# Row scatter and row gathers issued column by column behind block pairs, and second-half routing begun ahead of the first pair

## The chip, the cores and the metric

The kernel runs on one core of a Trainium2 chip. Its engines work side by side and wait for each other on semaphores: TensorE (PE, matrix multiplies), VectorE (DVE) and ScalarE (ACT, elementwise work), GpSimd (POOL), and SyncE (SP), which here only issues DMAs. GpSimd issues DMAs too, the indirect ones, whose row addresses come out of a table in on-chip memory. The metric is device time in microseconds of one execution; it is given as the median of three timed runs.

## The reference, cut to what matters

Two mixture-of-experts (MoE) feed-forwards stand before and behind a two-layer retention block. In all three the input is normalised first.

```python
def moe(hidden):                          # 4096 tokens of 256
    flat = hidden.reshape(4096, 256)
    probs = softmax(flat @ router_w + router_bias)     # 16 experts
    top_w, top_i = top_k(probs, 2)
    norm_w = top_w / (sum(top_w) + 1e-6)
    combine = sum(one_hot(top_i, 16) * norm_w[..., None], axis=1)
    routed = combine[:, 15:16] * flat                  # expert 15 is the identity
    for e in range(15):
        y = silu(flat @ gate_w[e]) * (flat @ up_w[e]) @ down_w[e]
        routed = routed + combine[:, e:e + 1] * y
    gate = causal_conv(hidden, conv_w)                 # 3 taps
    shared = silu(gate) * (hidden @ shared_up_w) @ shared_down_w
    return shared + routed

x = x + 0.5 * moe(layernorm(x))
x = x + retention_block(layernorm(x))     # 2 layers: projections, retention, feed-forward
x = x + 0.5 * moe(layernorm(x))
```

## The kernel before, in words

One program does both MoE layers and the retention block between them. Tiles of the first MoE have names that begin with `a_`, those of the second with `b_`, those of the retention block with `l_`; the code of the two MoE layers is the same. `x_sb` holds the activations on the chip.

An MoE layer works on its 4096 tokens in two halves of 16 columns; a column is 128 tokens, one to a partition. **Routing** of a half takes softmax and top-2 on DVE, then counts on PE (`count`, 17 small matmuls in one accumulation behind a clearing one) how many tokens each expert has, and DVE works out of the counts at which row of a DRAM buffer (`rows`) each token is to stand, so that the tokens of one expert lie side by side in blocks of 128 rows. The result is the index table `pos_i`, and the semaphore `placed` says that it is there. For the second half this runs as a generator `later` of seven pieces (plan, plan, place, place, weigh, block table, block table), of which DVE takes one behind the work of each block pair.

**Scatter.** GpSimd writes each column of normalised tokens twice (top-2) into `rows`, one indirect DMA for each: 32 for a half, L804. That of the second half waits only for `placed` and for the buffer's clearing.

**Block pairs.** The experts' work is a loop of 46 pairs of blocks; pairs 0 to 22 are of the first half, 23 to 45 of the second. For pair n: SP loads it (`load_block`, L470, four pairs ahead), PE transposes it (`turn_x`, L1284, two pairs ahead), ACT and DVE split it into a high and a low part (L650, L1009), PE multiplies it by the gate and up weights in three passes (`gateup`, L83 to L85, into `gu_ps`), ACT applies the gate (L658), DVE forms the product (`product`, L1017, whose semaphore is `h_done`), PE transposes the product (L1305), ACT and DVE split it (L664, L1023), PE does the down projection of it one pair later, ACT copies the result out of PSUM (`take_y`, L670), and SP stores it into `rows` (`store_y`, L476). ACT's `take_y` of a pair waits until the store of the pair two before it has left the buffer.

SP is one queue in order. In iteration q it issues the load of pair q+4 and then the store of pair q-3. The load of pair 23, the first of the second half, waits for all the second half's scatters; behind it on SP stand the load's own iteration's store, that of pair 16, and all that follows. In the first MoE, SP's queue also holds stores of weights (`low_dram`) in iterations 28 to 42 and three stores of `x`.

**Gathers ("picks").** When all stores of the first half have landed, GpSimd gathers the results of column c, two indirect DMAs each (L813), into a ring of 8 columns (6 in the second MoE), and DVE adds them into `x_sb` (`combine`, L1029), one column behind the product of each pair from n = 28 (`COMBINE_FROM`) on. From the ring's length on, a pick waits until `combine` has freed its slot.

So each engine's order is written out by hand, and what the change touches is: GpSimd's second scatter and its picks of the first half, DVE's order around `low_x(0)` and `low_x(1)` (which lead to the first product), and PE's order around `turn_x(0)`.

## Time and profile before

| what | value |
|---|---|
| median of 3 timed runs | 1405.84 us (1404.09 to 1406.28) |
| the profiled execution: its span | 1579.5 us |
| busy in the profiled span: PE | 1351.4 us (86%) |
| DVE | 1011.0 us (64%) |
| ACT | 614.6 us (39%) |
| POOL | 571.9 us (36%) |
| HBM traffic over the span | 95 GB/s |

The table puts two different things side by side. The time by which the kernel is judged is the first line. All durations and starts of single instructions come from one execution under the profiler, and that one took 173.7 us longer than the median. "Released by" in the profile is the instruction or DMA on whose semaphore an engine waited last. The end of a matmul is modelled; that of the other engines' instructions is recorded. PE is busy for most of the span; what follows is read in stretches, for the two MoE parts and the part between have different limits.

### The profile page before, as it was taken

The page shows a single profiled execution, that of the slowest core. Times are in us where ns is not written, and L with a number is a line of the kernel's source. Part 1 is how long each engine was busy: PE and PEld are TensorE (multiplying, and loading weights), DVE is VectorE, ACT ScalarE, POOL GpSimd, SP SyncE. Part 2 cuts the span into 40 slices and gives each one's busy share as a digit, 9 for nine tenths or more (in the row PEclk, how much of TensorE's full clock was granted, in tenths as well). Part 3 has the DMA queues.
Part 4 walks back from the last instruction along what each step waited for, and adds up shares of the span by engine and source line. Part 5 has one row for each costly group of instructions (what it writes and reads, how often), then busy time and mean ns, then how long its engine had stood idle before and what let it go on. Part 6 is the DMA issues. An engine that isn't in the chain of part 4 may idle for free.

```text
span 1579.5 us, 30698 instructions
## 1 busy us (share of the span) xinstructions
PE 1351.4 (86%) x11824; PEld 1104.9 (70%) x11824; DVE 1011.0 (64%) x2391; ACT 614.6 (39%) x1034; POOL 571.9 (36%) x460
## 2 busy tenths in 40 slices
PE   6871968876999999999998999999999676496885
PEld 3461968644788888888886888888887446496753
DVE  5661536658977877777768778797787453253623
ACT  5630635422333433343344334424455262263410
POOL 0726033352342323224424443364343704304252
PEclk9975979989999999999999999999999788698998
DMA  9963559650000000000010000000002463355542
GB/s 326 372 213 122 174 175 321 206 190 23 28 2 2 1 2 1 1 2 32 8 58 1 1 15 2 15 15 14 2 28 89 167 229 131 124 181 171 156 150 90
DMA packets 113867, 151.63 MB, mean 96 GB/s; under 512 B 12224, under 2 KB 96192, under 8 KB 113728
## 3 DMA queue, kind: packets, MB, share of 16 engines
q1 hardware_dynamic: 99328, 114.02, 21.8%
q0 software_dynamic: 12288, 33.57, 6.6%
q8 instruction: 99, 1.62, 0.4%
q10 hardware_dynamic: 2112, 2.10, 0.4%
q14 instruction: 40, 0.33, 0.1%
HBM read 78.21 MB, written 71.43 MB: 95 GB/s over the span
## 4 chain that ended last, share of the span: by engine, by line
PE 53%; DVE 16%; another core or an unknown queue 8%; issue 2%; ACT 2%; POOL 0%; DVEq 0%; ACTq 0%
PE l_w_ps L83 8%; PE l_w_ps L85 7%; PE l_w_ps L84 7%; DVE l_probs L2221 4%; PE l_banks L2505 3%; PE l_rm_ps L2537 2%; PE l_banks L83 2%; PE l_banks L84 2%; PE l_banks L85 2%; DVE l_f_lo L2252 2%; PE l_rm_ps L2530 2%; DVE l_full L2174 1%; PE b_gu_ps L83 1%; PE b_t_ps L1284 1%
## 5 line engine op out<-in xcount | busy, mean ns | idle before, releaser
L2221 DVE TENSOR_TENSOR l_probs<-l_banks,l_past 128x512 f32<-128x512 f32 x256 | 160.1, 684 | 29.8 <-PE l_banks L2505 29.7
L1964 ACT ACTIVATE l_act_f<-l_w_ps,l_ffn_b 128x512 f32<-128x512 f32 x120 | 82.7, 690 | 169.0 <-PE l_w_ps L85 163.9
L83 PE MATMUL l_w_ps<-l_w_hi,l_f_hi 128*128 128x256 f32 x496 | 143.6, 290 | 2.6 <-DVE l_f_lo L2252 2.4
L84 PE MATMUL l_w_ps<-l_w_lo,l_f_hi 128*128 128x256 f32 x496 | 139.6, 281 | 0.0
L85 PE MATMUL l_w_ps<-l_w_hi,l_f_lo 128*128 128x256 f32 x496 | 139.5, 281 | 0.0
L2059 POOL TENSOR_TENSOR l_g_lo<-l_q,l_g_hi 128x1024 fp32r<-128x1024 f32 x16 | 39.1, 2447 | 266.9 <-ACT l_g_hi L1955 266.9
L813 POOL DMA_INDIRECT b_picked<-rows,b_pos_i x64 | 61.1, 955 | 137.4 <-DMA rows<-b_yb 88.5
L83 PE MATMUL l_w_ps<-l_b_hi,l_w_hi 128*128 128x512 f32 x240 | 102.2, 426 | 0.3 <-ACT l_f_hi L1965 0.3
L83 PEld LDWEIGHTS l_w_ps<-l_w_hi,l_f_hi 128*128 128x128 f32 x496 | 93.3, 188 | 8.8 <-issue 8.7
L2252 DVE TENSOR_TENSOR l_f_lo<-l_act_f,l_f_hi 128x512 fp32r<-128x512 f32 x128 | 85.9, 703 | 18.5 <-ACT l_f_hi L1965 18.4
L2046 POOL TENSOR_TENSOR l_q_wide<-l_q,l_pair_mask 128x1024 f32<-128x1024 f32 x32 | 60.1, 1899 | 103.7 <-DVE l_q L2189 100.0
L804 POOL DMA_INDIRECT rows<-a_xn,a_pos_i x64 | 66.3, 1036 | 83.9 <-DVE a_pos_i L969 64.9
L85 PE MATMUL l_w_ps<-l_b_hi,l_w_lo 128*128 128x512 f32 x240 | 94.7, 394 | 0.0
L84 PE MATMUL l_w_ps<-l_b_lo,l_w_hi 128*128 128x512 f32 x240 | 94.5, 394 | 0.0
L84 PEld LDWEIGHTS l_w_ps<-l_w_lo,l_f_hi 128*128 128x128 f32 x496 | 93.5, 188 | 0.0
L85 PEld LDWEIGHTS l_w_ps<-l_w_hi,l_f_lo 128*128 128x128 f32 x496 | 93.4, 188 | 0.0
L1965 ACT ACTIVATE l_f_hi<-l_w_ps,l_ffn_b 128x512 fp32r<-128x512 f32 x120 | 81.8, 681 | 0.0
L1943 ACT ACTIVATE l_std<-l_mv,eps 128x4 f32<-128x4 f32 x47 | 13.6, 298 | 174.4 <-DVE l_mv L2144 170.7
L2537 PE MATMUL l_rm_ps<-l_probs,l_v_wide 128*32 128x128 f32 x2048 | 78.9, 275 | 2.8 <-DVE l_v_wide L2210 2.8
L2067 POOL TENSOR_TENSOR x_sb<-x_sb,l_bias 128x1024 f32<-128x1024 f32 x32 | 77.2, 2414 | 0.0
L2505 PE MATMUL l_banks<-l_q_wide,l_kT 32*128 32x256 f32 x1024 | 74.2, 401 | 1.0 <-POOL l_q_wide L2046 1.0
L2154 DVE TENSOR_SCALAR l_xn<-x_sb,l_mv,l_rstd 128x256 f32<-128x256 f32 x128 | 69.8, 606 | 1.2
(432 smaller groups left out, 4053.0 us busy)
## 6 DMA issues: line engine op xcount, KB each, us to landing
rows<-a_zeros SPq DMA_DIRECT2D x14, 1024.0 KB, 10.7
a_xb<-rows SPq DMA_DIRECT2D x46, 256.0 KB
rows<-a_yb SPq DMA_DIRECT2D x46, 256.0 KB
b_xb<-rows SPq DMA_DIRECT2D x46, 256.0 KB
rows<-b_yb SPq DMA_DIRECT2D x46, 256.0 KB
a_w_in<-in_moe_w SPq DMA_DIRECT2D x15, 384.0 KB, 10.2
low_dram<-a_w_lo SPq DMA_DIRECT2D x15, 384.0 KB
b_w_lo<-low_dram SPq DMA_DIRECT2D x15, 384.0 KB
```

What stands on the lines that cost most here:

```text
L83: tensor.matmul(out, w_hi, x_hi, start=start, stop=False)
L84: tensor.matmul(out, w_hi, x_lo, start=False, stop=False)
L85: return tensor.matmul(out, w_lo, x_hi, start=False, stop=stop)
L804: pool.indirect_dma_start(own_rows[b], bass.IndirectOffsetOnAxis(ap=pos_i[:, b, k, c:c + 1], axis=0), normal(START[b] + c), None).then_inc ...
L1964: nc.scalar.activation(act_f[:, f, :], hidden_ps(b, f), ACT.Gelu, bias=ffn1_b[:, b.layer, f:f + 1]).then_inc(act_done, 1)
L1965: nc.scalar.activation(f_hi[:, f, :], hidden_ps(b, f), ACT.Gelu, bias=ffn1_b[:, b.layer, f:f + 1]).then_inc(f_hi_done, 1)
L2067: pool.tensor_tensor(tile, tile, bias[:, row:row + 1, :].broadcast_to([P, SUB, D]), ALU.add).then_inc(done, 1)
L2154: last = dve.tensor_scalar(dst(s), tile_of(t, s), mv[:, s, 0:1], rstd[:, s:s + 1], ALU.subtract, ALU.mult)
L2221: dve.tensor_tensor(probs[c % 2][:, r * w:(r + 1) * w].rearrange("p (h n) -> p h n", n=P), banks[:, r, :].rearrange("p (h n) -> p h n", n= ...
L2252: dve.tensor_tensor(f_lo[:, f, :], act_f[:, f, :], f_hi[:, f, :].bitcast(F32), ALU.subtract).then_inc(f_lo_done, 1)
L2505: last = pe.matmul(banks[:, r, g * PH * P:(g + 1) * PH * P], kT[rows, g, t], q_wide[rows, g, :, t], start=True, stop=True)
L2537: last = pe.matmul(ret_ps[r * QUAD:(r + 1) * QUAD, g * P:(g + 1) * P], v_wide[:, c, g * NQ + r, i:i + PH, :].rearrange("p i x -> p (i x)") ...
```

## The change

Three edits, the same in both MoE layers.

1. GpSimd's scatter of column c of the second half waits for `h_done` of 2 + 19c//16. The semaphore counts finished products, so the 16 columns stand behind products 1, 2, 3, 4, 5, 6, 8, 9, 10, 11, 12, 14, 15, 16, 17 and 18.
2. GpSimd's pick of column c of the first half waits for `h_done` of 27 + 18c//16: behind products 26, 27, 28, 29, 30, 31, 32, 33, 35, 36, 37, 38, 39, 40, 41 and 42. The order of DVE's `combine` is as it was: column c behind product 28+c.
3. The count of the second half on PE moves from behind `turn_x(2)` of pair 0 to ahead of `turn_x(0)`. DVE takes the two plan pieces ahead of `low_x(0)` and `low_x(1)`, then two pieces of `later` for each of the first two pairs and one after that, so that `placed` of the second half comes behind product 0 and not behind product 3.

```diff
+            def paced_scatter(c):
+                pool.wait_ge(h_done, 2 + (PAIR0[1] - 4) * c // PARTS[1])
+
+            def paced_pick(c):
+                pool.wait_ge(h_done, COMBINE_FROM - 1 + (NPAIRS - COMBINE_FROM) * c // PARTS[0])
+
             def scatter(b):
                 pool.wait_ge(placed, b + 1)
...
                 for c in range(PARTS[b]):
+                    if b == 1:
+                        paced_scatter(c)
                     for k in range(2):
...
                 own = c - START[b]
+                if b == 0:
+                    paced_pick(c)
                 for k in range(2):
...
                 later = rest()
+            next(later)
             low_x(0)
+            next(later)
             low_x(1)
...
                 low_h(n)
-                next(later, None)
+                for _ in range(2 if n < 2 else 1):
+                    next(later, None)
...
                 shared_in(2)
+            count(1)
             if begins:
                 pe.wait_ge(dve_lo_done, PIECES)
             turn_x(0)
...
                 if n + 2 < NPAIRS:
                     turn_x(n + 2)
-                if n == 0:
-                    count(1)
```

What stands in a row on GpSimd, in the first MoE, from the first half's scatter on. Before (32 scatters of the first half, 32 of the second, then the picks; the waits are the semaphores' names):

```order
L804 DMA rows<-a_xn,a_pos_i 7936x256 [waits a_cleared0,a_placed]
L804 DMA rows<-a_xn,a_pos_i 7936x256 x31
L804 DMA rows<-a_xn,a_pos_i 7936x256 [waits a_cleared1,a_placed]
L804 DMA rows<-a_xn,a_pos_i 7936x256 x31
L813 DMA a_picked<-rows,a_pos_i 128x256 [waits a_scattered11,y_kept0,a_scattered10,y_kept1,a_scattered01,a_scattered00]
L813 DMA a_picked<-rows,a_pos_i 128x256 x15
L813 DMA a_picked<-rows,a_pos_i 128x256 [waits a_x_done]
L813 DMA a_picked<-rows,a_pos_i 128x256
```

Now (the lines L804 and L813 are L812 and L823), the same stretch up to the second half's third column:

```order
L812 DMA rows<-a_xn,a_pos_i 7936x256 [waits a_cleared0,a_placed]
L812 DMA rows<-a_xn,a_pos_i 7936x256 x31
L812 DMA rows<-a_xn,a_pos_i 7936x256 [waits a_h_done,a_cleared1,a_placed]
L812 DMA rows<-a_xn,a_pos_i 7936x256
L812 DMA rows<-a_xn,a_pos_i 7936x256 [waits a_h_done]
L812 DMA rows<-a_xn,a_pos_i 7936x256
L812 DMA rows<-a_xn,a_pos_i 7936x256 [waits a_h_done]
L812 DMA rows<-a_xn,a_pos_i 7936x256
```

Each column is now two DMAs behind a wait of its own, and the picks read likewise: two DMAs behind `a_h_done`, from the ninth column on behind `a_h_done,a_x_done`.

PE at the start of the second MoE's pairs, before: `shared_in(2)` (L415, L420), then the transposes of pairs 0 and 1 (L1284), then the shared expert's down projection (L427). (In the second MoE the waits carry semaphore names of the first, which are used again; `a_cleared0` here is the one that says that DVE has finished `b_both`, the routing's picks.)

```order
L1230 MATMUL b_low_ps<-ident,b_lgT_last 128x128 x3
L415 MATMUL b_gu_ps<-b_xT_first,b_w_sh 128x512 [waits a_low_kept,a_weight_in9,a_weight_in10]
L415 MATMUL b_gu_ps<-b_xT_first,b_w_sh 128x512 x5
L420 MATMUL b_gu_ps<-b_xT_first,b_w_sh 128x512 x2
L1284 MATMUL b_t_ps<-ident,b_xb 128x128 [waits a_weight_in10,a_halo_done]
L1284 MATMUL b_t_ps<-ident,b_xb 128x128 x3
L1284 MATMUL b_t_ps<-ident,b_xb 128x128 [waits a_weight_in10,a_xT_done]
L1284 MATMUL b_t_ps<-ident,b_xb 128x128 x3
L427 MATMUL b_acc_ps<-b_w_sh,b_sh 128x256 [waits a_zeroed,a_low_kept]
```

Now (L1240 is L1253, L1284 is L1297):

```order
L415 MATMUL b_gu_ps<-b_xT_first,b_w_sh 128x512 x5
L420 MATMUL b_gu_ps<-b_xT_first,b_w_sh 128x512 x2
L1253 MATMUL b_low_ps<-b_blank,b_ones 128x255 [waits a_cleared0]
L1254 MATMUL b_low_ps<-b_both,b_tri 128x240
L1256 MATMUL b_low_ps<-b_both,b_ones 128x240
...
L1256 MATMUL b_low_ps<-b_both,b_ones 128x15
L1297 MATMUL b_t_ps<-ident,b_xb 128x128 [waits a_weight_in10,a_halo_done]
L1297 MATMUL b_t_ps<-ident,b_xb 128x128 x3
L1297 MATMUL b_t_ps<-ident,b_xb 128x128 [waits a_weight_in10,a_xT_done]
```

The count, with its wait for `b_both`, now stands ahead of the first pair's transposes.

DVE at the same place of the first MoE, before (L1009 is `low_x`, L1017 the product, L1023 `low_h`, L947 to L949 the first plan piece):

```order
L1003 SCALAR_TENSOR_TENSOR x_sb<-a_acc_ps,x_sb 128x1024 [waits a_s_acc_done]
L1009 TENSOR_TENSOR a_bx_lo<-a_t_ps,a_bx_hi 128x512 [waits a_x_hi_done] x2
L1017 TENSOR_TENSOR a_bh<-a_bg,a_gu_ps 128x256 [waits a_gate_done]
L1009 TENSOR_TENSOR a_bx_lo<-a_t_ps,a_bx_hi 128x512 [waits a_gu_done,a_x_hi_done]
L1023 TENSOR_TENSOR a_bh_lo<-a_low_ps,a_bh_hi 128x256 [waits a_h_hi_done]
L947 TENSOR_SCALAR a_nb_i<-a_low_ps 128x15 [waits a_pre_done]
```

Now (each line ten higher):

```order
L1013 SCALAR_TENSOR_TENSOR x_sb<-a_acc_ps,x_sb 128x1024 [waits a_s_acc_done]
L957 TENSOR_SCALAR a_nb_i<-a_low_ps 128x15 [waits a_pre_done]
L958 TENSOR_SCALAR a_nb_i<-a_nb_i 128x15 [waits a_route_step]
L959 CAST a_nb<-a_nb_i 128x15 [waits a_route_step]
L1019 TENSOR_TENSOR a_bx_lo<-a_t_ps,a_bx_hi 128x512 [waits a_x_hi_done,a_route_step]
L961 TENSOR_TENSOR a_scratch<-a_lists,a_nb 128x225
L963 TENSOR_REDUCE a_first<-a_scratch 128x15 [waits a_route_step]
L966 SCALAR_TENSOR_TENSOR a_slots<-a_first,a_low_ps 128x16x15 [waits a_route_step]
L1019 TENSOR_TENSOR a_bx_lo<-a_t_ps,a_bx_hi 128x512 [waits a_x_hi_done,a_planned]
L1027 TENSOR_TENSOR a_bh<-a_bg,a_gu_ps 128x256 [waits a_gate_done]
```

The six plan operations stand ahead of and between the two `low_x` that the first product waits for.

## Rows read from the trace of the kernel before

**Rows 1.** The page's first line: the profiled span and its instructions.

```profile
span 1579.5 us, 30698 instructions
```

**Rows 2.** Busy time per engine in four stretches (a:b in us, their length, engines' busy time).

```profile
core 0: us, PE busy (x) PEld busy (x) DVE busy (x) ACT busy (x) POOL busy (x), PEclk, DMA share, GB/s
112.00:163.00 51.00, 17.48 (x105) 16.22 (x104) 10.22 (x24) 7.95 (x18) 31.36 (x32) 0.63 0.38 129
163.00:210.00 47.00, 46.88 (x395) 46.03 (x394) 25.10 (x49) 30.68 (x66) 0.00 (x0) 1.00 0.58 181
345.00:1175.00 830.00, 803.84 (x8507) 672.23 (x8510) 648.48 (x1506) 308.23 (x448) 309.99 (x188) 0.99 0.04 13
1319.00:1370.00 51.00, 15.79 (x97) 14.78 (x96) 9.21 (x23) 7.43 (x16) 31.17 (x32) 0.64 0.36 128
```

**Rows 3.** Timeline of POOL: start, duration, instruction, idle time before it and its releaser.

```profile
112.85 0.96 POOL L804 DMA_INDIRECT rows<-a_xn,a_pos_i  x1 [25.12 <-DVE a_pos_i L969]
...
152.70 0.96 POOL L804 DMA_INDIRECT rows<-a_xn,a_pos_i  x1 [0.30 <-issue]
...
210.48 0.98 POOL L813 DMA_INDIRECT a_picked<-rows,a_pos_i  x1 [56.81 <-DMA rows<-a_yb]
```

**Rows 4.** Timeline of DVE: products (a: pairs 4, 8, 11, 24, 28; b: 4, 8), first combine.

```profile
112.58 0.42 DVE L1017 TENSOR_TENSOR a_bh<-a_bg,a_gu_ps 128x256 f32<-128x256 f32 x1
...
162.58 0.42 DVE L1017 TENSOR_TENSOR a_bh<-a_bg,a_gu_ps 128x256 f32<-128x256 f32 x1 [2.08 <-ACT a_bg L658]
...
171.25 0.42 DVE L1017 TENSOR_TENSOR a_bh<-a_bg,a_gu_ps 128x256 f32<-128x256 f32 x1 [0.76 <-ACT a_bg L658]
...
208.87 0.42 DVE L1017 TENSOR_TENSOR a_bh<-a_bg,a_gu_ps 128x256 f32<-128x256 f32 x1 [0.92 <-ACT a_bg L658]
...
237.94 0.42 DVE L1017 TENSOR_TENSOR a_bh<-a_bg,a_gu_ps 128x256 f32<-128x256 f32 x1 [2.08 <-ACT a_bg L658]
...
240.05 0.48 DVE L1029 SCALAR_TENSOR_TENSOR x_sb<-a_picked,a_wk,x_sb 128x256 f32<-128x256 f32 x1
...
1319.59 0.42 DVE L1017 TENSOR_TENSOR b_bh<-b_bg,b_gu_ps 128x256 f32<-128x256 f32 x1
...
1371.01 0.42 DVE L1017 TENSOR_TENSOR b_bh<-b_bg,b_gu_ps 128x256 f32<-128x256 f32 x1 [2.08 <-ACT b_bg L658]
```

**Rows 5.** Timelines of PE and ACT: pair 6's last gate-and-up matmul, and its gate.

```profile
118.19 0.28 PE L85 MATMUL a_gu_ps<-a_w_hi,a_bx_lo 128*128 x1
127.79 0.38 ACT L658 ACTIVATE a_bg<-a_gu_ps 128x256 f32<-128x256 f32 x1 [5.57 <-remote]
```

**Rows 6.** Three longest pieces of the chain that ended last: start, length, what.

```profile
313.28 15.53 another core or an unknown queue
1242.20 27.56 another core or an unknown queue
1526.49 21.68 another core or an unknown queue
```

**Rows 7.** Timelines of SP and ACT: two stores of block results, and one copy from PSUM.

```profile
172.58 0.63 SPq L476 DMA_DIRECT2D rows<-a_yb  x1
207.24 0.46 SPq L476 DMA_DIRECT2D rows<-a_yb  x1
171.95 0.60 ACT L670 ACTIVATE a_yb<-a_acc_ps 128x512 f32<-128x512 f32 x1
```

**Rows 8.** Busy time in two stretches of the spaced picks, columns as in Rows 2.

```profile
250.00:268.00 18.00, 15.73 (x128) 15.07 (x129) 12.32 (x26) 9.44 (x22) 10.01 (x12) 1.00 0.99 342
1441.00:1485.00 44.00, 35.29 (x270) 32.49 (x269) 25.22 (x54) 20.99 (x46) 18.94 (x20) 0.98 0.65 187
```

**Rows 9.** Timelines of PE and DVE: second MoE's start and count, and a place piece.

```profile
1301.76 0.48 PE L427 MATMUL b_acc_ps<-b_w_sh,b_sh 128*128 128x256 f32 x1 [2.24 <-DVE b_sh L991]
...
1307.08 0.27 PE L1240 MATMUL b_low_ps<-b_blank,b_ones 128*128 128x255 bf16 x1
1307.19 0.27 PE L1241 MATMUL b_low_ps<-b_both,b_tri 128*128 128x240 bf16 x1
1307.30 1.12 PE L1243 MATMUL b_low_ps<-b_both,b_ones 128*128 128x240 bf16 x16
...
108.65 0.75 DVE L965 TENSOR_TENSOR a_picks<-a_picks,a_slots 128x256 f32<-128x256 f32 x2
```

## The prediction

> **What bounds the kernel now.** I read the page's first line first and set it against the median. The profiled span is 1579.5 us [rows 1], the median 1405.84 us, 173.7 us apart. Before anything is subtracted from the span, that difference has to be found in the trace, for a stall that only the profiled execution has can't be recovered in the timed ones.
>
> The busy time by stretches shows where it can lie [rows 2]. In the retention block (345 to 1175 us) PE is busy for 803.84 of 830 us, in 163 to 210 us for 46.88 of 47. Nothing like 174 us fits there. In 112 to 163 us PE is busy for only 17.48 of 51 us, while POOL, with 32 instructions in it, is issuing; 1319 to 1370 us is the same picture in the second MoE.
>
> POOL's timeline tells what is issued: the second half's scatter begins at 112.85 and its last DMA starts at 152.70, 0.96 us each with 0.30 us between [rows 3]. DVE's timeline gives the price: pairs 4 to 8 take from 112.58 to 162.58 us, 50.0 us. The quiet pace is (208.87 - 171.25) / 13 = 2.89 us a pair, so four pairs are worth 11.6 us and 38.4 us are lost. In the second MoE it is 1371.01 - 1319.59 - 11.6 = 39.8 us, and at the first picks of the first MoE 237.94 - 208.87 - 11.6 = 17.5 us [rows 4]. What stalls isn't a unit that is short: pair 6's last gate-and-up matmul starts at 118.19 us and takes 0.28, but the gate that waits for it starts at 127.79, 9.3 us later [rows 5]. PE's completion reaches its waiter late while POOL issues without a break. The chain of waits holds three more such holes, 15.5, 27.6 and 21.7 us, called "another core or an unknown queue" [rows 6].
>
> Sum: 38.4 + 39.8 + 17.5 + (15.5 + 27.6 + 21.7), and some 14 to 17 us more if the second MoE's first picks cost about what the first's do, is 175 to 178 us. That is the whole difference between span and median (173.7). So I read the timed runs as containing next to nothing of these stalls. The uncertainty of such a sum is some 25 us (whether all of each hole would close), and that is the most that can be left in the timed runs.
>
> The Trainium skill speaks against this reading: Runtime: NRT & Kernel Launch, in "The ~15µs preamble/postamble breakdown", puts a profile's total about 6 us above the executed time, whatever the kernel. By it the stalls would be in the timed runs; here the two are 173.7 us apart, so this case does not agree.
>
> **The change part by part.** *What it removes.* In the profile, four bursts are spread out, the two scatters and the first picks of both MoE. Two scatters of 38 to 40 us become 17 pairs each, in which two DMAs of 1.27 us lie in every pair of 2.9; at up to 0.7 us a pair that leaves 12 us. The span should fall by 2 x 27 for the scatters and some 12 for the picks, to about 1512 us (1480 to 1550). In the timed runs, of the at most 25 us that may be left, the change touches the four bursts, some 110 of the 175 us, thus 0 to 16; I take 5, since the sum closes to within a few us. Term: -5.
>
> *Scatter behind pairs.* Nothing wants the scatter before load 23, so its price is at its end. The last column waits for product 18 (call it T). Its two DMAs end 0.42 + 2 x 1.27 - 0.3 = about 2.7 us behind T, and the data lands later; the store of a block result shows 207.24 to 210.48, 3.24 us from issue to the pick that waits for the landing [rows 3, 7]. An indirect DMA need not take all of that behind its end; I take 2 us, so load 23 leaves SP at T + 4.6 and the store of pair 16 behind it. In the quiet pace a store leaves 1.33 us behind its product (172.58 against 171.25) [rows 4, 7]; here the store of pair 16, due at about T, leaves 4.6 us late and lands near T + 7. ACT's `take_y` of pair 18 needs that buffer; it starts 0.70 us behind the next product (171.95 against 171.25) [rows 4, 7], that is T + 2.9 + 0.7 = T + 3.6. It waits 3.4 us, and the gate and high parts behind it on ACT wait too; PE is two steps ahead by the transposes and the double buffers give back about 0.8 us. That is 2.6 us; before, load 23 stood behind a scatter that was done long ago, but the same store crossed the same queue for perhaps 0.3. Term: +2.3 for each MoE, +4.6 (bounds 0 to 8: nothing if the landing comes at once, 4 each if it takes the full 3.2 us).
>
> *Picks behind pairs.* Column c < 8 is issued two pairs ahead of its `combine`, which stands at 240.05 us, 2.11 us behind product 28 [rows 4]; two pairs are 5.8 us, against 2.2 for the issue and 3.24 for the landing, so it just holds. For c >= 8 there is one pair of lead: product n, then 0.42 + 2.2 for the issue, then the landing, then the combine, ahead of product n+2 on DVE. With 3.2 us for the landing the way is 0.4 + 2.2 + 3.2 = 5.8 plus the combines' 0.5, 6.3 against 5.8 us for two pairs. Late by half a microsecond each in quiet queues. But in the first MoE the queues aren't quiet here: in 250 to 268 us the DMA share is 0.99 at 342 GB/s, with the weights' and `x` stores; in the second it is 0.65 [rows 8]. At a landing of 4 to 4.5 us the cycle of two pairs grows to about 7 us, 0.6 us a pair over eight pairs, +5 (bounds 0 to 8). Before, the ring let POOL run six to eight columns ahead, so this is a wait that was not there. In the second MoE I take +1 (0 to 3). Behind the waiting `combine` on DVE stand the next product and `low_x`, so it is PE's loss as well. Before, these same DMAs went out in one burst plus one per freed slot, so no traffic is removed.
>
> *Start of the pairs.* In the first MoE PE sits idle ahead of its first transposes, and the count goes into that gap: 0. In the second, PE is at work up to the shared expert's down projection at 1301.76 and then starts pair 0. The count takes from 1307.08 to 1308.42 us [rows 9], 1.34 us, 2.7 at the lower clock level, and stands now ahead of `turn_x(0)`: +2.1. It also waits for DVE's `b_both`; what queues behind that wait is the first transposes, and I take no more for it. Two plan pieces on DVE ahead of the first product cost +1.5; the place piece of 0.75 us [rows 9] and its kin, now off the pairs 1 to 4, give back 1.2 if they had delayed a product. Together +3 with what the doubled pieces at pair 0 and 1 cost (bounds 0 to 4). Wherever the 2.9 us of a pair hide them, this is 0.
>
> **The sum.** 4.6 + 5 + 1 + 3 - 5 = +8.6, so 1405.84 + 8.6 = 1414.4 us.
>
> **The rivals.**
> *A: the bursts cost time in the timed runs too, and the waits are covered.* For it: the stalls follow POOL's bursts so exactly that nothing in the trace marks them as the profiler's, and my sum can be off by 25 us. Against it: the sum meets the difference. It gives 16 off, +4 for the start: about 1394 us. The full version, all of the profile's gain of 67 us in the timed runs, gives 1339; it needs the 174 us to come from somewhere that [rows 2] leaves no room for. It is the skill's rule above.
> *B: nothing on the path moves.* The landings are near 1 us behind the issue, the store of pair 16 keeps its slack, the picks land in time, the start's count fills an idle PE. Then the terms are +0 to +2 and -0 to -2: 1406 us. For it: PE waits for DVE with slack in many pairs; against it: one pair of lead is less than issue and landing by the rows.
> *C: waits at the upper bounds.* 8 + 8 + 3 + 4 and no relief: +23, 1429 us. It decides if the landing under a DMA share of 0.99 is over 5 us.
> *D: the opposite sign by the DMA queues alone.* The Trainium skill, DMA: Bandwidth & Descriptors, "Issuing engines are not separate DMA queues", has all issuers share the same 16 engines. A scatter of 32 DMAs in one burst then delays the loads of pairs 8 to 10; [rows 2] shows a share of only 0.38 in that stretch, so spreading it wins nothing, and no chance is set apart for it beyond A's.
>
> **How the numbers follow.** Forecast (a net loss of 3 to 16 us) 0.46, A 0.24 and its full version 0.03, B 0.17, C 0.10. A measurement of this kernel can tell about 0.2%, 2.8 us, from no change. The range takes in A and all but the end of C: 1394 to 1426 us leaves out about 0.2. Faster than 1403: 0.27 + a sliver of B's, 0.28; within 0.2%: 0.17; slower: 0.55. The forecast's own range is 1409 to 1422.
>
> **What would show it.** After the change POOL's timeline should show two DMAs behind each product of pairs 1 to 18, and products there at 3.5 us or less from each other and no hole of 12 to 30 us. At pair 18 to 19 one gap of 5 to 6 us should stand, released by the store's landing, on ACT. In pairs 36 to 43 of the first MoE `combine` should be released by the pick's DMA. The start of the second MoE's first product should be some 3 us later. The forecast is wrong if the median falls along with the span (then A), if the pick's landing is no releaser (then B), or if the gap at pair 18 is absent.

## The result: 26 us slower on the chips that were timed

The changed kernel takes 1431.99 us (median of 4, 1428.09 to 1436.4) and the kernel before, beside it, 1406.06 us. The ratio is 1.0184, 95% interval 1.0157 to 1.0211. The prediction had slower by 8.6 us, 1414.4, with a range up to 1426: the sign was right, the size was a third of the measured one, and the time lies outside the range.

The changed kernel's profile fits its times: its span is 1433.1 us. That of the kernel before stood 174 us over its times ([rows 1]). So the kernel before was profiled once more (run e5 below), and this time its span is 1404.6 us. That clean profile is what the changed one has to be set against. The page's first lines, changed kernel, then the kernel before profiled again:

```profile
span 1433.1 us, 30719 instructions
```

```profile
span 1404.6 us, 30698 instructions
```

The busy time by stretches answers [rows 2]. Columns: from:to and length in us, busy time (instructions) of PE, PE's weight loads, DVE, ACT and POOL, granted clock (1.00 is full speed), DMA share, GB/s. The second half's scatter in the first MoE, in the kernel before, profiled again:

```profile
112.00:154.00 42.00, 41.51 (x347) 40.54 (x346) 25.08 (x53) 27.14 (x59) 31.24 (x32) 1.00 0.84 264
```

The same burst of 32 DMAs is there, 31.24 us of POOL, and PE is busy for 41.51 of 42 us beside it. In [rows 2] it was 17.48 of 51. The burst as such stalls nothing on this chip; on which chips it does comes further down.

Where the 26 us come from is read off DVE's products (the semaphore that all the new waits use). The changed kernel: products 4 and 8 of the first MoE, 19 and 21, 28 and 45, then of the second `b_both`, products 4, 19, 21, 28 and 45:

```profile
111.83 0.42 DVE L1027 TENSOR_TENSOR a_bh<-a_bg,a_gu_ps 128x256 f32<-128x256 f32 x1 [0.80 <-ACT a_bg L658]
123.73 0.42 DVE L1027 TENSOR_TENSOR a_bh<-a_bg,a_gu_ps 128x256 f32<-128x256 f32 x1 [1.04 <-ACT a_bg L658]
156.01 0.42 DVE L1027 TENSOR_TENSOR a_bh<-a_bg,a_gu_ps 128x256 f32<-128x256 f32 x1 [0.79 <-ACT a_bg L658]
168.37 0.42 DVE L1027 TENSOR_TENSOR a_bh<-a_bg,a_gu_ps 128x256 f32<-128x256 f32 x1 [1.66 <-ACT a_bg L658]
188.94 0.42 DVE L1027 TENSOR_TENSOR a_bh<-a_bg,a_gu_ps 128x256 f32<-128x256 f32 x1 [1.00 <-ACT a_bg L658]
254.20 0.42 DVE L1027 TENSOR_TENSOR a_bh<-a_bg,a_gu_ps 128x256 f32<-128x256 f32 x1 [1.27 <-ACT a_bg L658]
1222.35 0.43 DVE L942 TENSOR_TENSOR b_both<-b_picks 128x256 bf16<-128x256 f32 x1
1242.72 0.42 DVE L1027 TENSOR_TENSOR b_bh<-b_bg,b_gu_ps 128x256 f32<-128x256 f32 x1 [0.88 <-ACT b_bg L658]
1286.74 0.42 DVE L1027 TENSOR_TENSOR b_bh<-b_bg,b_gu_ps 128x256 f32<-128x256 f32 x1 [0.76 <-ACT b_bg L658]
1298.36 0.42 DVE L1027 TENSOR_TENSOR b_bh<-b_bg,b_gu_ps 128x256 f32<-128x256 f32 x1 [1.53 <-ACT b_bg L658]
1318.92 0.42 DVE L1027 TENSOR_TENSOR b_bh<-b_bg,b_gu_ps 128x256 f32<-128x256 f32 x1 [1.18 <-ACT b_bg L658]
1374.60 0.42 DVE L1027 TENSOR_TENSOR b_bh<-b_bg,b_gu_ps 128x256 f32<-128x256 f32 x1 [1.83 <-ACT b_bg L658]
```

The kernel before, profiled again, at the same places (these answer [rows 4]):

```profile
111.82 0.42 DVE L1017 TENSOR_TENSOR a_bh<-a_bg,a_gu_ps 128x256 f32<-128x256 f32 x1
123.67 0.42 DVE L1017 TENSOR_TENSOR a_bh<-a_bg,a_gu_ps 128x256 f32<-128x256 f32 x1 [0.98 <-ACT a_bg L658]
155.57 0.42 DVE L1017 TENSOR_TENSOR a_bh<-a_bg,a_gu_ps 128x256 f32<-128x256 f32 x1 [0.76 <-ACT a_bg L658]
163.77 0.42 DVE L1017 TENSOR_TENSOR a_bh<-a_bg,a_gu_ps 128x256 f32<-128x256 f32 x1 [0.72 <-ACT a_bg L658]
184.88 0.42 DVE L1017 TENSOR_TENSOR a_bh<-a_bg,a_gu_ps 128x256 f32<-128x256 f32 x1 [1.00 <-ACT a_bg L658]
242.02 0.42 DVE L1017 TENSOR_TENSOR a_bh<-a_bg,a_gu_ps 128x256 f32<-128x256 f32 x1 [0.95 <-ACT a_bg L658]
1208.10 0.43 DVE L932 TENSOR_TENSOR b_both<-b_picks 128x256 bf16<-128x256 f32 x1
1225.32 0.42 DVE L1017 TENSOR_TENSOR b_bh<-b_bg,b_gu_ps 128x256 f32<-128x256 f32 x1
1269.82 0.42 DVE L1017 TENSOR_TENSOR b_bh<-b_bg,b_gu_ps 128x256 f32<-128x256 f32 x1 [0.80 <-ACT b_bg L658]
1275.99 0.42 DVE L1017 TENSOR_TENSOR b_bh<-b_bg,b_gu_ps 128x256 f32<-128x256 f32 x1 [0.73 <-ACT b_bg L658]
1296.77 0.42 DVE L1017 TENSOR_TENSOR b_bh<-b_bg,b_gu_ps 128x256 f32<-128x256 f32 x1 [1.03 <-ACT b_bg L658]
1347.28 0.42 DVE L1017 TENSOR_TENSOR b_bh<-b_bg,b_gu_ps 128x256 f32<-128x256 f32 x1 [0.95 <-ACT b_bg L658]
```

| stretch | before | changed | difference |
|---|---|---|---|
| first MoE, product 4 to 8 (a burst before) | 11.85 | 11.90 | 0.05 |
| first MoE, product 19 to 21 (the scatter's end) | 8.20 | 12.36 | 4.2 |
| second MoE, product 19 to 21 | 6.17 | 11.62 | 5.5 |
| first MoE, product 28 to 45 (the picks) | 57.14 | 65.26 | 8.1 |
| second MoE, product 28 to 45 | 50.51 | 55.68 | 5.2 |
| second MoE, `b_both` to product 4 (the start) | 17.22 | 20.37 | 3.2 |

The last five are some 26 us; the timed difference is 25.9, that of these two spans 28.5. Each column is one execution, and the profiled one of the changed kernel took 2.9 us more than its median (1434.92).

**The hole at the scatter's end**, in the changed kernel's timelines of POOL, SP, ACT and PE:

```profile
153.86 0.96 POOL L812 DMA_INDIRECT rows<-a_xn,a_pos_i  x1 [0.58 <-DVE a_bh L1027]
155.13 0.96 POOL L812 DMA_INDIRECT rows<-a_xn,a_pos_i  x1 [0.30 <-issue]
...
158.84 0.36 SPq L470 DMA_DIRECT2D a_xb<-rows  x1
159.25 0.47 SPq L476 DMA_DIRECT2D rows<-a_yb  x1
...
162.30 0.60 ACT L670 ACTIVATE a_yb<-a_acc_ps 128x512 f32<-128x512 f32 x1 [5.67 <-DMA rows<-a_yb]
...
163.77 0.51 PE L83 MATMUL a_acc_ps<-a_w_hi,a_bh_hi 128*128 x1 [4.92 <-DVE a_bh_lo L1033]
```

Product 18 starts at 153.16 us. The last column's two DMAs end on POOL at 156.09 (155.13 + 0.96); load 23 leaves SP at 158.84, 2.75 us behind them, and the store of pair 16 behind it at 159.25. ACT's copy of a result out of PSUM stands for 5.67 us until that store has landed, and PE stands for 4.92. Then PE's clock is down, in the stretch behind the hole (columns as above):

```profile
164.00:168.00 4.00, 4.00 (x23) 4.00 (x23) 1.09 (x2) 0.92 (x3) 0.00 (x0) 0.59 0.75 258
```

The granted clock is 0.59 where it is 1.00 in the undisturbed stretch, near the lower of the two levels (1.2 of 2.4 GHz), after PE was idle. Product 20 starts at 163.54, so the pair behind the hole takes 4.83 us (163.54 to 168.37), where a pair ahead of it took 2.85 (153.16 to 156.01). So a hole of 4.7 us (7.53 less 2.85) costs 6.7.

**The picks**, in the list of waits of the changed kernel from 188 to 254 us (total, times, longest), a line that the kernel before doesn't have at all in the same pairs:

```profile
DVE x_sb L1039 <- DMA a_picked<-rows,a_pos_i: 9.3, 6, 2.5
```

and the second MoE's, from 1318 to 1375 us:

```profile
DVE x_sb L1039 <- DMA b_picked<-rows,b_pos_i: 5.2, 6, 1.4
```

One of them in POOL's and DVE's timelines, column 8, released by product 35 (start 212.02 us):

```profile
213.19 0.95 POOL L823 DMA_INDIRECT a_picked<-rows,a_pos_i  x1 [4.40 <-DVE a_bh L1027]
214.44 0.95 POOL L823 DMA_INDIRECT a_picked<-rows,a_pos_i  x1 [0.30 <-issue]
...
220.46 0.48 DVE L1039 SCALAR_TENSOR_TENSOR x_sb<-a_picked,a_wk,x_sb 128x256 f32<-128x256 f32 x1 [2.49 <-DMA a_picked<-rows,a_pos_i]
```

1.17 us from the product's start to the issue, 2.2 us for two DMAs, 5.07 us from the end of the issue to the data: 8.44 us for a lead of one pair.

The waits cost more than their own length, for the clock goes down with them. Products 28 to 45 of the first MoE, the kernel before (profiled again), then the changed one:

```profile
184.90:242.00 57.10, 50.95 (x406) 47.73 (x405) 37.80 (x82) 30.95 (x67) 23.39 (x24) 1.00 0.92 326
188.90:254.20 65.30, 54.51 (x407) 52.12 (x406) 38.64 (x83) 31.84 (x68) 26.91 (x28) 0.92 0.85 292
```

The same 406 or 407 matmuls keep PE busy for 54.51 us at a granted clock of 0.92 and for 50.95 at 1.00. So 3.6 of the 8.1 us are PE running slower, and the rest is PE standing.

**The second MoE's start.** PE in the changed kernel, then in the kernel before (`b_both` starts on DVE at 1222.35 and 1208.10):

```profile
1222.83 0.28 PE L1253 MATMUL b_low_ps<-b_blank,b_ones 128*128 128x255 bf16 x1 [2.51 <-DVE b_both L942]
...
1224.04 1.07 PE L1297 MATMUL b_t_ps<-ident,b_xb 128*128 128x128 f32 x8
```

```profile
1207.16 1.33 PE L1284 MATMUL b_t_ps<-ident,b_xb 128*128 128x128 f32 x8 [1.10 <-DMA b_xb<-rows]
```

PE now stands for 2.51 us until `b_both` is there, and the first pairs' transposes stand behind that wait and the count. They start 1.69 us behind `b_both`, where they started 0.94 us ahead of it: 2.6 us later. Product 0 starts 7.41 us behind `b_both` and not 4.95, and the rest of the 3.2 us is lost by product 4.

### The profile page after: what moved, and what is told of

The parts are those of the page before. It is cut to its first block and busy times, and to the rows that moved or that the text cites. A ratio compares the mean times of both kernels' runs of the same rounds, so it can differ in the third digit from the quotient of the medians.

```text
span 1433.1 us, 30719 instructions
## 1 busy us (share of the span) xinstructions
PE 1325.4 (92%) x11824; PEld 1093.8 (76%) x11824; DVE 1013.0 (71%) x2391; ACT 617.1 (43%) x1034; POOL 574.9 (40%) x460
## 5 line engine op out<-in xcount | busy, mean ns | idle before, releaser
L812 POOL DMA_INDIRECT rows<-a_xn,a_pos_i x64 | 65.8, 1029 | 86.6 <-DVE a_pos_i L979 40.1
L823 POOL DMA_INDIRECT b_picked<-rows,b_pos_i x64 | 62.6, 978 | 74.0 <-issue 33.1
## 6 DMA issues: line engine op xcount, KB each, us to landing
rows<-a_zeros SPq DMA_DIRECT2D x14, 1024.0 KB, 12.4
```

The source lines that it names most:

```text
L812: pool.indirect_dma_start(own_rows[b], bass.IndirectOffsetOnAxis(ap=pos_i[:, b, k, c:c + 1], axis=0), normal(START[b] + c), None).then_inc ...
```

## The experiments

All ratios are to the kernel before on the same chip. Up to e8 and from e14 on that is a chip on which it takes 1405 to 1407 us.

### One edit at a time

Run e1 is the kernel before with the paced scatter only:

```diff
+            def paced_scatter(c):
+                pool.wait_ge(h_done, 2 + (PAIR0[1] - 4) * c // PARTS[1])
...
                 for c in range(PARTS[b]):
+                    if b == 1:
+                        paced_scatter(c)
                     for k in range(2):
```

> The kernel before with the second half's scatter behind block pairs and nothing else. Theory (the wait at the scatter's end): in the changed kernel the pairs 18 to 20 take 12.4 us in the first MoE and 11.6 in the second where two pairs take 5.7, since the store of pair 16 stands on SP behind the load of pair 23; so 6.7 + 5.9 = 12.6 us slower than before, about 1418.5 us, with the same hole. Rival (the loss is the picks' or the start's): within 3 us of before, 1406. If the burst had cost time in the timed runs and pacing gives it back, it would be under 1418 by that much.

Measured: 1416.68 us, ratio 1.0074 (1.0057 to 1.0091), +9.9 us. The holes are there: products 19 to 21 take 13.1 and 12.4 us. It is less than the 12.6 expected because the kernel before has a small hole of its own at this place (8.20 us above where two quiet pairs take 5.7). Its burst starts with product 4 and ends at 152.76 us, 2.8 us ahead of product 19; load 23 leaves SP at 154.28 and the store behind it at 154.69, and ACT stands for 3.05 us until that store has landed. The end of the scatter is a cost by itself.

Run e2 is the kernel before with the paced picks only:

```diff
+            def paced_pick(c):
+                pool.wait_ge(h_done, COMBINE_FROM - 1 + (NPAIRS - COMBINE_FROM) * c // PARTS[0])
...
                 own = c - START[b]
+                if b == 0:
+                    paced_pick(c)
                 for k in range(2):
```

> The kernel before with the first half's picks behind block pairs and nothing else. Theory: the rest of the 26 us, less the start's 1.5, is the picks': about 11 to 12 us slower, 1417 to 1418 us. Rival (the scatter's end is all of the loss, and the picks only stand where they stood): within 3 us of before. The prediction's own term for it was 6 us, 1412.

Measured: 1415.03 us, 1.0050 (1.0032 to 1.0067), +8.3 us. A loss of its own, less than the 11 to 12 expected. In its trace products 28 to 45 take 59.46 us in the first MoE and 53.83 in the second, 2.3 and 3.3 more than before, and 19 to 21 of the first take 9.80, 1.6 more.

Run e3 is the changed kernel without both kinds of waits, so only the routing's move is left:

```diff
-                    if b == 1:
-                        paced_scatter(c)
...
-                if b == 0:
-                    paced_pick(c)
```

> The kernel before with the second half's count and plan pieces ahead of the first pair, both scatters and picks as before. Theory: from the end of the routing's picks to product 4 the second MoE takes 20.35 us in the changed kernel and 18.91 in the one before, and the first MoE's product 4 comes 0.8 us earlier; so +0.6 us, 1406 to 1408. The prediction's term was +3, 1409. Rival: the second scatter's burst now begins three pairs earlier, which moves where it collides; if that matters, it is over 3 us either way.

Measured: 1408.18 us, 1.0019 (1.0007 to 1.0030), +1.4 us. Its trace shows both halves of it: products 19 to 21 of the first MoE take 5.8 us, so the small hole of before is gone (the burst starts at 103.95 us and not at 112.08), and from `b_both` to product 4 the second MoE takes 20.2 us, not 17.2. It is also the first trace with all bursts in it and no stall: span 1406.1 us.

The three add up to 19.6 us, 6 less than the change. The routing's move brings its gain at the same place as the paced scatter puts its hole, so the two together lose that gain (2.5 us). What is left, some 4 us, is within the sum of the intervals. The traces put it in the picks: the same waits cost 2.3 us in the first MoE by themselves (e2), and 8.1 in the traces of the changed kernel and of e4 below. Each of these is one execution, and why they cost more beside the other edits isn't shown.

### Mending the late ends

Run e4 is the changed kernel with the scatter's columns spread less far:

```diff
-                pool.wait_ge(h_done, 2 + (PAIR0[1] - 4) * c // PARTS[1])
+                pool.wait_ge(h_done, 2 + (PAIR0[1] - 8) * c // PARTS[1])
```

> The changed kernel with the scatter's columns spread up to product 15 and not 18 (19 in the rule replaced by 15). Theory: the data of the last column lands 2.75 us behind its DMA's end, about product 17, before load 23 is due on SP, so the holes at pairs 18 to 20 close: 12.6 us faster than the changed kernel, 1432 - 12.6 = 1419 us. Rival (pairs are slowed by spread-out DMAs as such, or the hole only moves): 1428 to 1434, or a hole of the same size elsewhere.

Measured: 1417.59 us, 1.0079 (1.0063 to 1.0095), 14.4 us less than the changed kernel, and products 19 to 21 take 5.9 and 5.8 us. Spreading the 32 DMAs among the pairs costs nothing that shows; that the last ones come late does.

Run e6 is the changed kernel with the picks' rule replaced:

```diff
-                pool.wait_ge(h_done, COMBINE_FROM - 1 + (NPAIRS - COMBINE_FROM) * c // PARTS[0])
+                pool.wait_ge(h_done, COMBINE_FROM - 1 + c)
```

> The changed kernel with the pick of column c behind product 26 + c for all c, so that each has two pairs of lead over its combine (before: two for c < 8, one from there). Theory (the picks' term is the one pair of lead): the combine's waits for its pick's DMA go from 9.3 us to 1 or 2 in the first MoE and to nothing in the second, so some 8 to 11 us faster than the changed kernel, 1421 to 1424 us. Rival (the picks' waits or their spread-out traffic cost time whatever the lead): 1430 or more.

Measured: 1422.02 us, 1.0109 (1.0089 to 1.0130), 10 us less than the changed kernel. The wait for the pick's DMA, 9.3 us over six waits in the changed kernel, is in its trace from 189 to 247 us:

```profile
DVE x_sb L1039 <- DMA a_picked<-rows,a_pos_i: 3.6, 4, 1.6
```

and in the second MoE's pairs the line is gone. Products 28 to 45 take 57.76 and 50.02 us, where the kernel before takes 57.14 and 50.51. Lead is the cause; in the first MoE, where the DMA share is 0.92 in the kernel before, two pairs are still a little short.

Run e7 has both mends.

> The changed kernel with both mends: the scatter spread only up to product 15, the picks with two pairs of lead. Theory (both losses are late ends): 1417.6 - 8 to 11 = 1407 to 1410 us, level with the route-only kernel's 1408.2. Rival (spreading itself costs): 1413 or more. Should bursts cost anything in the timed runs, it would come out under 1405.

Measured: 1408.89 us, 1.0025 (1.0012 to 1.0038), as the theory had it, and once more as run e15 on another chip, 1.0021 (1.0007 to 1.0035). Of 26 us, 22 are gone.

### The routing's move where it helps, and a version that loses nothing

Run e8 is the kernel before with the routing's move in the first MoE only:

```diff
+            if begins:
+                next(later)
             low_x(0)
+            if begins:
+                next(later)
             low_x(1)
...
-                next(later, None)
+                for _ in range(2 if n < 2 and begins else 1):
+                    next(later, None)
...
             if begins:
+                count(1)
                 pe.wait_ge(dve_lo_done, PIECES)
...
-                if n == 0:
+                if n == 0 and not begins:
                     count(1)
```

> The kernel before with the routing's move in the first MoE alone; the second MoE, both scatters and all picks as before. Theory: the move gains 4 us in the first MoE, where before load 23 stood on the scatter's end (a hole of 4.1 us at pairs 19 to 20 in the picks-only kernel's trace, none in the route-only's), and costs 3.1 in the second MoE's start; so without the latter 1406.8 - 4 = 1402.5 to 1405 us, faster than both kernels. Rival: the move is worth nothing in either, 1406 to 1408.

Measured: 1403.8 us, 0.9992 (0.9982 to 1.0002). Against before this can't be told from no change; against e3 (1.0019) it is 0.27% less, the cost of the second MoE's start. Run e17 puts the same restriction into the mended kernel of e7.

> The changed kernel with the scatter up to product 15, picks with two pairs of lead, and the routing's move in the first MoE alone. Theory: the second MoE's start gives back 3.1 us of the other mended kernel's 1.0023 of before, so at the 1406 level 1405 to 1407 us, 1.000 of before (rival, if the move's cost is not there: 1.002); at the 1580 level about 12 to 20 us under the changed kernel's 0.958, so 0.945 to 0.950 of before, which would make it level with before on one kind of chip and faster on the other.

Measured: 1405.54 us, 0.9993 (0.9982 to 1.0003), 0.3% (4 us) less than e7 and e15. So the start's term is 3 to 4 us, and paced scatters and picks cost nothing that shows once their ends are early enough. It doesn't beat the kernel before either, on these chips.

### Why the scatter's end costs: a store behind a load

In the hole two things are late, load 23 itself and the store of pair 16 behind it. The next two runs change SP's order alone, in the changed kernel (e9) and the kernel before (e10). The loads of pairs 23 to 25 go behind the store of pair 18; they leave SP no earlier than in the changed kernel.

```diff
-                if q + XB < NPAIRS:
+                first = PAIR0[1] - XB
+                if q + XB < NPAIRS and not first <= q < first + 3:
                     load_block(q + XB)
                 if q >= LAG:
                     store_y(q - LAG)
+                if q == first + 2:
+                    for late_load in range(3):
+                        load_block(PAIR0[1] + late_load)
```

> The changed kernel with one order changed on SP: the loads of pairs 23, 24 and 25 are issued together behind the store of pair 18, so that no store stands behind the wait for the scatter; the scatter ends when it did. Theory (the hole is the store of pair 16 standing behind load 23): the holes at pairs 18 to 20 (6.7 and 5.9 us over two quiet pairs) shrink to 0 to 1 us, so 1432 - 11 = 1419 to 1422 us. Rival (the hole is load 23 itself coming too late for its transposes, or the scatter's last DMAs): the load leaves SP no earlier than now, so the hole stays or moves two pairs on, and the time stays at 1429 to 1434.

> The kernel before with the same order on SP, nothing else. Theory: the clean profile of before has such a hole once, in the first MoE, pairs 19 to 21 in 8.2 us and not 5.7; it closes, so 2.5 us faster than before, 1403 to 1404 us. Rival (late load): 1405 to 1407, as before, or slower if the three loads in a row delay the stores behind them.

Both fell on a chip on which the kernel before takes 1581.06 us and not 1406: e9 took 1503.33 us there (0.9518, 0.9488 to 0.9549), e10 1581.9 (1.0012, 0.9991 to 1.0033). So they answered another question first (next section). Repeated together with the changed kernel they fell on a second chip of that kind, as e12 and e13:

> The changed kernel with the loads of pairs 23 to 25 issued behind the store of pair 18, as before. Theory (head of line on SP): 10 to 12 us faster than the changed kernel on the same chip, whichever level: 1419 to 1422 us at the lower, 1503 at the upper; the traces' holes at pairs 18 to 20 are gone, as the first run of it already showed (2.9 us a pair there). Rival (late load): level with the changed kernel.

> The kernel before with the same order on SP. At the lower level the theory says 1403 to 1404 us (its hole of 2.5 us in the first MoE closes); rival 1405 to 1407 us. At the upper level there is no hole, because the stalls give the scatter time to end: level with before, as measured once (1.0012).

Measured: 1507.04 us (0.9522, 0.9470 to 0.9574) and 1577.79 us (0.9999, 0.9967 to 1.0031), the changed kernel beside them 1512.11. The 5 us between the first and the last are within their intervals. At the 1406 us level both were measured as e14 and e16:

> The changed kernel with the loads of pairs 23 to 25 behind the store of pair 18, once more. If before is at 1406 us on this chip, the theory (a store stands behind load 23) gives 1419 to 1422 us, 1.010 of before, and the rival (the load itself is late) 1.018. If before is at 1580 us, 0.952 again.

> The kernel before with the same order on SP. At the 1406 level the theory gives 2.5 us less than before (0.998), the rival no difference. At the 1580 level no difference.

Measured: e14 1418.79 us, 1.0092 (1.0070 to 1.0115), 13 us less than the changed kernel; e16 1404.22 us, 0.9987 (0.9974 to 1.0000). Products 18 to 21 of the first MoE in the trace of e14:

```profile
153.83 0.42 DVE L1031 TENSOR_TENSOR a_bh<-a_bg,a_gu_ps 128x256 f32<-128x256 f32 x1 [0.76 <-ACT a_bg L662]
156.64 0.42 DVE L1031 TENSOR_TENSOR a_bh<-a_bg,a_gu_ps 128x256 f32<-128x256 f32 x1 [0.74 <-ACT a_bg L662]
159.95 0.42 DVE L1031 TENSOR_TENSOR a_bh<-a_bg,a_gu_ps 128x256 f32<-128x256 f32 x1 [1.02 <-ACT a_bg L662]
162.76 0.42 DVE L1031 TENSOR_TENSOR a_bh<-a_bg,a_gu_ps 128x256 f32<-128x256 f32 x1 [0.78 <-ACT a_bg L662]
```

The load leaves SP at 159.84 us, 6.0 us behind product 18 (it was 5.7), and there is no hole. In the second MoE products 19 to 21 take 6.29 us, not 11.62. The late load costs next to nothing (products 21 to 28 take 21.93 and 20.62 us, in the changed kernel 20.57 and 20.56); the store that stood behind it did. The holes are closed in e12's trace too (6.14 and 6.13 us, and 11.92 and 10.88 in e11's, the changed kernel on that chip). For the kernel before the same order shows in the trace (products 19 to 21 in 6.0 us, not 8.2) and is on the edge of what the times can tell.

### The second kind of chip

> The kernel before, unchanged, profiled again. The route-only kernel has both scatters and the first picks in bursts as before, and its profiled span is 1406.1 us with no stall. Theory: the stalls of the first profile belong to that one execution and not to the bursts; a second one has a span of 1403 to 1410 us, and a hole of 4 us at pairs 19 and 20 of the first MoE only. Rival: this kernel's own timing makes the stalls whenever it is profiled, and the span is 1550 to 1600 us again.

Measured: span 1404.6 us, the execution 1406.42 us, no stall anywhere. By this alone the stalls of the first profile looked like an accident of that one execution. The chips of e9 to e13 show that they are not: there the kernel before has medians of 1581 and 1578 us and no timed run of 34 under 1566. Profiled there was only its variant with SP's order changed (e10, e13), and that has the pattern of [rows 2]: in e10 PE is busy for 15.29 of the 51 us from 112 to 163.

> The changed kernel, unchanged, beside the kernel before on one chip. The kernel before has now shown two levels, 1406 us on two chips and 1581 us on a third, and its first profile (span 1579.5) is of the second level. Theory (the stalls are real executions on chips of one kind, and POOL's bursts make them): on a chip of the 1406 level this is 1430 us, 1.018 of before; on one of the 1581 level about 1503 + 11 = 1514 us or less, 0.95 to 0.96 of before, with the pairs 4 to 8 at 3 us each. Rival (the level has nothing to do with the bursts): 1.018 of before on either, 1610 us at the upper level.

Measured: 1512.11 us, 0.9582 (0.9529 to 0.9635). On this chip the change makes the kernel 4% faster. Two traces of that one chip, over the first MoE's pairs 4 and on. The kernel before with SP's order changed (e13; its second scatter is a burst as before):

```profile
112.00:154.00 42.00, 12.08 (x76) 10.88 (x74) 6.42 (x17) 4.79 (x10) 30.71 (x32) 0.66 0.41 137
```

The changed kernel (e11), the paced scatter, then the first half's scatter in the second MoE, which isn't paced:

```profile
112.00:154.00 42.00, 35.82 (x288) 33.89 (x288) 18.68 (x37) 22.37 (x51) 19.16 (x20) 1.00 0.70 221
1191.00:1235.00 44.00, 26.29 (x123) 16.48 (x121) 16.89 (x61) 9.65 (x19) 32.28 (x32) 0.78 0.44 158
```

and that same unpaced scatter in the changed kernel's profile of the other kind of chip:

```profile
1175.00:1219.00 44.00, 43.52 (x210) 27.68 (x209) 32.34 (x113) 30.29 (x51) 32.62 (x32) 1.00 0.85 319
```

With 32 DMAs back to back PE is busy for 12 of 42 us on the one kind of chip; with two for each pair for 36 of 42, where the changed kernel on the other kind has 40.8. Products 4 to 8 take 51.30, 12.89 and 11.90 us in these three traces, so spread DMAs still cost a little there. Where the changed kernel still bursts, it still stalls there (26 of 44 us), and on the other kind of chip the same code runs at 43.5 of 44. What differs between the chips isn't shown by any run.

> The changed kernel with the scatter up to product 15 and picks with two pairs of lead. At the 1406 level it was 1.0025 of before and should be again. At the 1580 level it spreads the bursts as the changed kernel does and lacks its late ends: 12 to 23 us faster than the changed kernel's 1512, so 1489 to 1500, 0.943 to 0.950 of before.

This one met the 1406 us level (result above), and so did e17, so whether a mended version keeps the gain on the other kind of chip was not measured.

## Why the prediction was right in sign and wrong in size

**The base.** It read the timed runs as nearly free of the stalls, from the sum of the holes against the 173.7 us. On chips of the 1406 us level that held: products 4 to 8 take the same 11.9 us in both kernels, and nothing was there to be relieved. The term of -5 us was therefore wrong; it should have been 0. The reason given, that only the profiled execution has the stalls, fell. A whole kind of chip has them, and the profile of before looks like one from such a chip (span 1579.5; 1577.5 in e10). On which chip it was taken isn't recorded. The step that failed is the one sentence "a stall that only the profiled execution has": the rows can't tell an overhead of profiling from a chip of another kind. The expected span of 1512 us is close to what e11 shows on such a chip (1504.1); the rival with the stalls in the timed runs put the gain at 67 us, and on such a chip it is 66 (1578.41 to 1512.11), from a base 173 us higher than the rival took. The prediction cited the Trainium skill, Runtime: NRT & Kernel Launch, "The ~15µs preamble/postamble breakdown", which puts a profile's total some 6 us above the executed time, and found that this case did not agree. But the rule is about one execution, and the 173.7 us lay between a span and the times of other executions. Of one execution the span, from first to last instruction, lies 1.8 us below the time: 1404.6 and 1406.42 in e5, 1577.5 and 1579.3 in e10. A profile's total in the rule's sense is shown by no run here. What the prediction took from the rule, that such stalls are in the execution's own time, is so.

**The scatter's end: mechanism right, term mis-sized.** The chain (last column, load 23, the store behind it, ACT's copy) is in the rows step by step, and e14 shows that it is the store. 4.6 us were forecast and 9.7 measured (4.2 + 5.5 read from the traces). ACT's wait was worked out as 3.4 us and is 5.67. Four steps were short, in the first MoE: the last DMA ends 2.93 us behind the product's start, not 2.7; the landing takes 2.75, not 2; the store leaves 0.4 us behind the load, which was put at nothing; and it lands 3.05 us later (159.25 to 162.30), not 2.4. The 0.8 us that the double buffers were to give back are there: ACT stands for 5.67 us and PE for 4.92. What was left out is the clock that falls while PE stands, 2 us for this hole. In the other direction the kernel before has a hole of 2.5 us here in the first MoE, which was put at 0.3. The rows could not show it: in the profile that they are from, the scatter ends ahead of product 8 ([rows 3, 4]).

**The picks: mechanism right, term mis-sized.** 6 us were forecast, 13.3 read from the changed kernel's trace (8.1 + 5.2). By themselves they are 5.6 us in e2's trace, of 8.3 by its time, so by themselves they are near the forecast, and how much of the 13.3 the combination adds isn't settled. The landing was taken as 4 to 4.5 us in the first MoE and is 5.07 for the column shown; the issue was put 0.42 us behind the product's start and comes at 1.17. The point from which the upper rival was to decide was "over 5 us", and that is what came. The clock was left out here too, 3.6 of the 8.1 us. In the second MoE 1 us was taken and 5.2 measured: one pair of lead is short even at a DMA share of 0.69 (1319 to 1375 us of the changed kernel).

**The start: right number, wrong path.** +3 were forecast, 3.2 read from the traces, 3 to 4 by e17 against e7 and e15. But the forecast made it up of the count on PE (+2.1) and the plan pieces on DVE (+1.5), and took nothing for the wait for `b_both`. The trace has PE standing 2.51 us in that wait; the count takes 1.2 us, from 1222.83 to 1224.04; and `low_x(0)` waits 0.60 us for ACT behind the first plan piece, so that piece delays nothing. That the number came out is luck. It isn't firm to a microsecond either: from `b_both` to product 4 the one mended kernel takes 21.9 us in e7's trace and 20.5 in e15's.

**The sum.** By the traces 9.7 + 13.3 + 3.2 - 0 = 26.2, where 4.6 + 6 + 3 - 5 = 8.6 was written. About 5 us each of the miss come from the scatter's end and from the relief that wasn't there, 7 from the picks. The rival C (all waits at their upper bounds, no relief, 1429 us) came nearest, and it had a chance of 0.10. Its number is in part luck: two of its bounds were passed (5.5 us for the second MoE's scatter against 4, 5.2 for its picks against 3), and the clock was in none of them.

## What to carry to other kernels

Work that was spread behind the steps of this loop cost nothing that showed while it ran, and its whole price at pieces that came too late for what wanted them. Set each such wait back from its consumer by the way to the issue, the issue and the landing, here 1.2 + 2.2 + 5 us at a nearly full DMA share, and one step of slack (the slack is advice; no run here had three pairs of lead). On a queue in order, look at what stands behind the instruction that now waits; the late load was nearly free, and the store behind it cost some 6 us a time. When a piece of work is moved ahead on an engine, look first at what it waits for: the count took 1.2 us and its wait 2.5. When a profile's span doesn't fit the times, have the kernel profiled and timed on another chip before either is explained: this change is 1.018 of before on one kind of chip and 0.958 on the other.

## What the runs showed of the hardware

The kernel before takes 1406 us on chips 1, 3, 10 and 12 and 1578 to 1581 us on chips 5 and 8; no timed run lies between 1412.4 and 1566.7. On the latter, work that PE has finished reaches its waiters late while GpSimd issues indirect DMAs back to back (1.26 us from one to the next): 9.3 us in [rows 5], and up to 14.4 us of standing on ACT in e13. With two DMAs to a pair, four pairs take 12.89 us there against 11.90. On the former the same burst beside the same work leaves PE busy for 41.51 of 42 us. And a hole of 4.7 us in PE's work cost 2 us more behind it, at a granted clock of 0.59.
